# Five unused matrix products ahead of a selection, and the last row's stores split over two queues, in a decoder block's mixing stage

## What is computed

```python
H_res = sinkhorn_log(H_res_logits)            # 50 iterations on a 4 x 4 matrix per token
H_res = (1.0 - g) * I + g * H_res
y = x_pre @ W_branch
x_mixed = jnp.einsum('btij,btjc->btic', H_res, x_streams)
y_distributed = jnp.einsum('btc,btn->btnc', y, H_post)
return (x_mixed + y_distributed).reshape(B, T, nC)
```

## Time and profile before

| what | before |
|---|---|
| median of three runs | 1187.41 us |
| the profiled execution's own time | 1188.75 us |
| its span, first to last instruction | 1186.9 us |
| TensorE (PE) busy | 1028.0 us, 87% |
| VectorE (DVE) busy | 907.4 us, 76% |
| ScalarE (ACT) busy | 599.3 us, 50% |
| GpSimd (POOL) busy | 448.0 us, 38% |
| mean granted TensorE clock | 0.937 of full |

### The profile page before, as it was taken

How to read it: one execution, slowest core, us unless ns; L and a number is a source line. 1 busy time by engine, 2 the same in 40 slices (tenths; PEclk the granted TensorE clock), 3 DMA queues, 4 the chain that set the end, 5 groups by cost and what they waited for, 6 DMA issues and landing times. The chain is left out here.

```text
span 1186.9 us, 23294 instructions
## 1 busy us (share of the span) xinstructions
PE 1028.0 (87%) x7874; PEld 762.4 (64%) x7874; DVE 907.4 (76%) x2830; ACT 599.3 (50%) x1787; POOL 448.0 (38%) x665
## 2 busy tenths in 40 slices
PE   5889999999999999999956999999899899833328
PEld 4667777777778777787745677776555565422215
DVE  6756876667866678666563787789999999899993
ACT  6624555435554455544464676775566554421215
POOL 0714433334332344333342675674443343103011
PEclk9989999999999999999968999999999999855759
DMA  9111111110111101110122133233222221119407
GB/s 378 44 43 41 38 60 60 54 48 18 60 60 60 42 18 59 60 60 26 43 109 107 54 101 101 79 98 111 76 94 76 76 92 48 40 36 338 124 4 192
DMA packets 47234, 95.71 MB, mean 81 GB/s; under 512 B 5952, under 2 KB 30400, under 8 KB 47168
## 3 DMA queue, kind: packets, MB, share of 16 engines
q1 hardware_dynamic: 47168, 94.91, 23.6%
HBM read 64.48 MB, written 27.26 MB: 77 GB/s over the span
## 5 line engine op out<-in xcount | busy, mean ns | idle before, releaser
L689 POOL TENSOR_TENSOR prob_G<-prob_G,rl 128x512 f32<-128x512 f32 x96 | 99.7, 1040 | 251.2 <-DVE rl L570 251.2
L436 ACT ACTIVATE prob_G<-prob_G,negm 128x128 f32<-128x128 f32 x384 | 148.8, 389 | 83.4 <-DVE negm L512 83.4
L291 PE MATMUL ps_qkv<-w_hi,xT_hi 128*128 128x512 f32 x384 | 156.4, 407 | 17.4 <-DVE prob_G L575 9.2
L292 PE MATMUL ps_qkv<-w_lo,xT_hi 128*128 128x512 f32 x384 | 151.1, 394 | 0.0
L293 PE MATMUL ps_qkv<-w_hi,xT_lo 128*128 128x512 f32 x384 | 150.9, 393 | 0.0
L365 PE MATMUL ps_qkv<-wo_hi,aT_hi 128*128 128x512 f32 x256 | 109.3, 427 | 0.0
L367 PE MATMUL ps_qkv<-wo_hi,aT_lo 128*128 128x512 f32 x256 | 103.2, 403 | 0.0
L366 PE MATMUL ps_qkv<-wo_lo,aT_hi 128*128 128x512 f32 x256 | 103.2, 403 | 0.0
L291 PEld LDWEIGHTS ps_qkv<-w_hi,xT_hi 128*128 128x128 f32 x384 | 72.7, 189 | 43.2 <-issue 20.2
L508 DVE TENSOR_TENSOR prob_G<-ps_s,mask 128x512 f32<-128x512 f32 x96 | 64.9, 676 | 43.5 <-PE ps_s L274 43.0
L537 DVE TENSOR_TENSOR xT_lo<-ps_t,xT_hi 128x512 fp32r<-128x512 f32 x16 | 11.1, 692 | 101.5 <-ACT xT_hi L475 101.5
(11 more groups left out here) (292 smaller groups left out, 2684.0 us busy)
## 6 DMA issues: line engine op xcount, KB each, us to landing
xin<-in_x SPq DMA_DIRECT2D x16, 512.0 KB, 3.3
xres<-in_x SPq DMA_DIRECT2D x16, 512.0 KB, 4.9
x<-xres SPq DMA_DIRECT2D x16, 512.0 KB, 2.7
c_xin<-x SPq DMA_DIRECT2D x16, 512.0 KB, 4.3
c_b_xres<-x SPq DMA_DIRECT2D x16, 512.0 KB, 3.2
rows_x<-c_row SPq DMA_DIRECT2D x64, 128.0 KB, 2.3
m_xm<-rows_x SPq DMA_DIRECT2D x16, 512.0 KB, 7.7
out<-m_ot SPq DMA_DIRECT2D x64, 128.0 KB, 2.2
```

What stands on the lines that cost most here:

```text
L291: nc.tensor.matmul(ps_qkv[:, n, :], xT_hi[:, k, :], w_hi[:, k, cols], start=k == 0, stop=False)
L292: nc.tensor.matmul(ps_qkv[:, n, :], xT_hi[:, k, :], w_lo[:, k, cols], start=False, stop=False)
L436: r = nc.scalar.activation(prob(g)[:, j, :], prob(g)[:, j, :], ACT.Exp, bias=negm[:, h:h + 1], accum_out=lsum[:, h:h + 1])
L689: nc.gpsimd.tensor_tensor(prob(g), prob(g), rl[:, g * GROUP:(g + 1) * GROUP].rearrange("p (j o) -> p j o", o=1).to_broadcast([P, GROUP, T] ...
```

## The change

It does two things in `mixing_phase`, and nothing is removed.

- TensorE, after `branch_part(5)` and before `select(one_b)`: wait for bank 3 to be free; wait for step 286 of chain `one_b` (`BASES[2] - 22`), issue three products of `sel_sb[:, 0, :]` (128 by 128) with the whole of `sel_sb` (128 by 512, f32) into bank 3; wait for step 303 (`BASES[2] - 5`), issue two more. Nothing reads the result; `branch_part(6)` overwrites it.
- The last row's four stores: SP issues the first two, and ScalarE, at the end of its list and after waiting for all parts of the last row, its own and VectorE's, issues the other two on its own queue.

```diff
-                for i in range(NS):
+                for i in range(NS if n < B - 1 else 2):
                     sp.dma_start(out[n].rearrange("(g t) d -> t g d", g=NS)[:, :, i * C:(i + 1) * C],
                                  ot[n][i * W:(i + 1) * W, :, :]).then_inc(stored[n % 2], 16)
...
                 if n == one_b.first_row:
                     branch_part(n)
+                    bank_free(NS * (n + 1) - BANKS)
+                    for step, count in ((BASES[2] - 22, 3), (BASES[2] - 5, 2)):
+                        pe.wait_ge(one_b.step, step)
+                        for i in range(count):
+                            nc.tensor.matmul(p_out[NS * (n + 1) % BANKS][:, :], sel_sb[:, 0, :],
+                                             sel_sb[:, :, :].rearrange("p g t -> p (g t)"), start=True, stop=True)
                     select(one_b)
...
             take_out(LAST - 2, B)
+            act.wait_ge(out_done, NS * LAST + 2 * (B - LAST))
+            act.wait_ge(out_by_dve, 2 * (B - LAST))
+            for i in range(2, NS):
+                nc.scalar.dma_start(out[B - 1].rearrange("(g t) d -> t g d", g=NS)[:, :, i * C:(i + 1) * C],
+                                    ot[B - 1][i * W:(i + 1) * W, :, :]).then_inc(stored[(B - 1) % 2], 16)
```

## The result

The changed kernel takes 1186.15 us (median of 20 runs, 1183.34 to 1189.71), the kernel before, run beside it, 1188.68 us (20 runs, 1184.54 to 1191.55). The ratio is 0.9978, with a 95% interval of 0.997 to 0.9986: 2.6 us faster, between 1.7 and 3.6. The profiled execution took 1184.40 us, and its span is 1182.6; the profiled execution of the kernel before took 1188.75, with a span of 1186.9.

A forecast was written before the change was run, and what follows sets the result against it. Time could be won in the relay's half-clock TensorE pieces (1147.75 to 1156.23) and the stores after 1182.68. Products -0.95 and stores -0.5 sum to -1.45 us: from 1187.41 to 1186.0, range 1183.4 to 1188.8.

The forecast's parts named there:

- slow-queue case: Final stores: ScalarE's queue is slower than SP's, +1.95 us, and with no clock gain 1189.4 us; chance 0.10.
- The cover of the products: TensorE's idle stretch, 1108.25 to 1147.75, hides every added product; waiting for the bank costs nothing.
- Step 5: VectorE's chain beside the added products: TensorE's reads could slow it, between nothing and 0.2 us, taken as +0.1.
- The rise: TensorE's clock rises in the first batch of three products, 5.1 us at half clock, or at the latest in the next.
- No rise: Clock stays half through all five products, selection 0.1 to 0.3 us late, stores make up for it: 1187.1; chance 0.06.
- The selection at full clock: Selection after the added products takes 1.04 us in place of 2.09, a term of -1.05 us.
- step 4: Around the selection TensorE idles 3.5 of 4.5 us: selection at full clock (-1.05 us), row 5 at half clock again.
- Lost before the selection: Clock falls while TensorE waits for the coefficients, so only the stores remain: 1187.0 us; chance 0.30.
- Row 5 at half clock: Behind the selection the clock falls again, so the 2.08 us of row 5 and its branch part stay.
- held: Clock stays full from the selection until row 5, winning all 3.13 us: 1183.9 us; chance 0.14.
- The stores: Last row's stores on two queues at the kernel's end: -0.5 us, bounds -0.95 and +1.95.
- the fall at row 5: Once the clock has fallen, it rises 4.2 to 4.7 us after row 5 begins, as before, leaving row 5's cost.

The follow-up runs named there:

- e2: The changed kernel's five products without its store change, all stores by SP, against the kernel before: 1183.81 us, ratio 0.9955.
- e3: Changed kernel with one more product before the selection and two more between selection and row 5: 1186.25 us, ratio 0.9972 to the kernel before.
- e6: The changed kernel once more, nothing altered, timed beside the kernel before: 1185.43 us, ratio 0.9973.
- e8: Changed kernel with all five products in one batch at step 286: 1186.75 us in a single run.
- e9: e3 with all stores by SP, plus unused products in TensorE's pauses ending the second stage: 1182.47 us, ratio 0.9938 to the kernel before.
- e7: Kernel before without added products, ScalarE issuing the last two stores of row 12, SP all of the last row: 1185.30 us, one run.

## Why the prediction was right, and where it was off

The direction, "the same" within 0.5% and the time (1186.0 against 1186.15) came out. That the time did so within 0.2 us is luck. The forecast counted from 1187.41, the median of three runs, and the kernel before has 1188.68 over 20, 1.3 us more. The gain was 1.1 us larger than forecast, and the two errors nearly cancel. The size did not quite come out: -1.45 us forecast, -2.6 measured, and the interval's upper end is -1.7. The range of the forecast, 1183.4 to 1188.8, was not worked out from its cases either: its own slow-queue case, 1189.4, lies outside it.

- **The cover of the products** held. They lie in idle time, nothing waits for the bank, and the chain's iteration is unchanged. Step 5's +0.1 us was wrong; it measured 0.0. So the 2.19 us of the earlier trace rows has another cause than TensorE's reads, and which is not known.
- **The rise** came in the first batch or the pause behind it in the changed kernel, e2, e3 and e6, and within the batch of five in e8: from 3.5 us after it began (e2) to 5.9 (the changed kernel), and 2.9 in e9, a wider spread than the 4.2 and 4.7 of the earlier trace rows. "No rise" was not seen.
- **The selection at full clock** (step 4): 1.17 us where I took 1.04, so the term was -0.92 in place of -1.05. "Lost before the selection", to which I gave 0.30, was not seen in four executions.
- **Row 5 at half clock** (step 4) is the step that failed. The profiled execution of the changed kernel went as forecast, but that was one of two outcomes: the clock was lost around row 5 in two of four executions and held in two. I gave "held" 0.14. The average of the products is -1.9 us where the sum had -0.95.
- **The stores**: the transfers gained 0.4 us as worked out, but the close of the kernel, which I had left out of the sum, takes 0.34 us more with a second queue. The term was -0.1 in place of -0.5. The Trainium skill ("Trainium Kernel Development and Optimization", Key Constraints) says that issuing from several engines saves the sequencer's issue time only. The traces agree: SP's last issue ends 0.89 us after the last take-out in place of 1.88, and no more than that is won.

With the measured terms the sum is -1.9 - 0.1 = -2.0 us, inside the interval of the result. The remaining 0.6 us is smaller than half the interval's width, and I have no cause to give for it.

The forecast's remark that the fall at row 5 would leave its cost as before held roughly: from row 5 to row 6 it is 4.87 us in e6 and 4.20 in the changed kernel, against 4.57 before. The rise did not come 4.2 to 4.7 us after row 5 began, as it said, but after 3.6 in the changed kernel and 5.2 in e6.

## What to carry to other kernels

Work without use on TensorE can pay when it stands in a pause right before work on the path. Close all the pauses of the relay, not only the first: with the changed kernel's products the clock held in two of four executions, with the pauses closed in five of five. Look for these places by the clock column of short stretches, in every stage. Here the place that the change left alone, at the end of the second stage, was worth more than the one it treated: 3.6 us and more in the medians, against 2.6. Where a clock can fall or not between executions of one schedule, forecast the mean over both outcomes, and never read a change of a few microseconds off one pair of profiles before the segments that it does not touch are subtracted.

## What was not expected of the hardware

- One and the same schedule of TensorE keeps its clock in one execution and loses it in another. In the second stage the same 1.17 us wait was followed by half clock in six of twelve executions (with e9, which leaves it open), at a cost of 1.7 us in the product group and 2 us or more for the stage.
- The clock can fall after work was taken up again: at 1147.92 in the changed kernel, 0.2 us into row 5, and in the middle of the selection in e8 (1147.34).
- A second hardware queue makes the close of the program 0.80 us long in place of 0.46, in seven of seven executions each, also in e7, where ScalarE issued its stores at 1171.35 and the last wait ended at 1182.7.
- Thirty-one microseconds of products on TensorE beside a chain of small VectorE operations changed the chain's pace by less than 0.01 us in 2.16.
